# A vision tower with a Mamba block and 16 experts: routing weights by DMA from a small table, multiplied in by GpSimd

## The chip, the cores and the metric

One core of a Trainium2 chip runs the whole program in one launch. The metric is the device time of one execution in microseconds (us). TensorE, VectorE (DVE), ScalarE (ACT), GpSimd (POOL) and SyncE (SP, which here only issues DMAs) each run their own queue in order and meet at semaphores.

## What is computed

The input is 32 images, 36 patches each, so 1152 tokens of 192 features after the patch embedding. A layer norm feeds a Mamba block (input projection with a gate, a selective scan over the 36 tokens of an image with 16 states for each of 384 channels, output projection, then a gated FFN of 512). A second layer norm feeds a mixture of experts:

```python
g = t @ gate_w.T + gate_b
vals, idx = jax.lax.top_k(g, K)            # K = 4 of E = 16
w = jax.nn.softmax(vals, axis=-1) / K
full_w = zeros((T, E)).at[arange(T)[:, None], idx].set(w)
h = einsum('th,ehf->tef', t, w1) + b1
h = _swiglu(h)        # min(glu, 7) * sigmoid(1.702 glu) * (clip(lin) + 1)
y = einsum('tei,eih->teh', h, w2) + b2
out = einsum('teh,te->th', y, full_w) * K
```

All 16 experts are computed for every token; the routing weight is zero for twelve of them. Everything is float32.

## The kernel before, in words

Features lie on the partitions, tokens on the free axis. The tokens are cut into four chunks of 8 images, T = 288 tokens. `schedule()` (L76) writes one order of steps by hand: A is the Mamba part of a chunk, B the experts of the chunk before it, and pieces of B are set ahead of named steps of A (`PIECES_BEFORE`, `DOWNS_BEFORE`). `run` (L360) goes through that order three times over: once with A alone for the first chunk, three times in a hardware loop with A of chunk c and B of chunk c-1, once with B alone for the last chunk. Each engine picks its own steps out of the same order, so an engine's queue is in this order whatever else is ready.

A has a scan of 24 steps of two halves each. A half is: TensorE spreads a row of B over the partitions (`spread`, L576), VectorE multiplies (L974) and scans (L983); GpSimd multiplies both halves of a step by C (`read`, L1212) into one of three buffers, and TensorE sums them (`collect`). A state buffer is used again three steps later.

B works on units. Two experts' 192 channels make three tiles of 128, so there are 24 units; the third of each pair has 64 channels of either expert. A unit has these steps:

- gate and linear: five matmuls each on w1 split in a high and a low part (`experts_up`, L692), the bias and minimum on VectorE (L1104), the bias on ACT, the clip on VectorE (L1112: SBUF to SBUF, in two buffers);
- mix: tanh on ACT, (tanh + 1) * gate on VectorE (L1120: two SBUF inputs, one buffer), the product `glu` with the clipped linear part on GpSimd (L1224: one buffer, so it waits for the unit before to be scaled);
- scale: TensorE copies the routing weights of the unit's expert to all 128 partitions in PSUM by a matmul with a selection matrix (`experts_scale`, L717: `pick_unit` times `mix_parts`), and VectorE multiplies `glu` by it into one of 12 `hid` tiles (L1129).

```python
pieces.append([("gate", u)] + ([("scale", u - 1)] if u else []))
pieces.append([("linear", u), ("mix", u)])
```

Each two units have three `down` steps of fp32 matmuls from `hid` by w2 into sums in PSUM, and `experts_finish` adds them to the residual. The order sets units 0 to 7 before the scan, 8 to 15 in it (the scales in it are of units 7 to 14) and 16 to 23 after it.

Before the units come topk (router logits and the four largest), weights (three transposes, ACT copies to `mix_w`, rounds to the upper rows of `mix_parts`, VectorE puts the rest into its lower rows, L1097) and start. The steps topk, weights, start, unit 0 and gate 1 with scale 0 stand ahead of A's `variance`, in which GpSimd takes the power -1/2 for the norms (`take_roots`, L1165 to L1167), after which VectorE makes `diag` (L915), TensorE spreads it and VectorE scales the features (L924, L927).

SP loads the patches of the next chunk in `center` (L445: 864 KB, into `x_patch`), and w1 of pair e+2 once the last linear of pair e is done (L453: 1152 KB, two buffers); it waits in its queue in the same order. In the first chunk ACT rounds `pick_unit` from a 576 KB load that lies in `hid` until then (L828, L479), and VectorE zeroes the other rows (L1149, L1150).

## Time and profile before

| | us |
|---|---|
| median of 3 runs | 804.27 (803.79 to 808.25) |
| the profiled execution | 805.15 |
| its span in the trace | 803.4 |
| TensorE busy | 634.8 (79%) |
| VectorE busy | 523.8 (65%) |
| ScalarE busy | 275.0 (34%) |
| GpSimd busy | 273.9 (34%) |
| DMA | 65.97 MB, mean 82 GB/s |
| mean granted TensorE clock | 0.881 of 2.4 GHz |

The trace lists every instruction with start and duration, what it waited for, and the clock that TensorE was granted (1.0 or 0.5, that is 2.4 or 1.2 GHz). Matmuls are pipelined, so their durations overlap and their sum is more than they cost; start to start is the measure. All matmuls come from the helper on L488 and all ACT instructions from L751, so they are told apart by the tiles that they write and read. Tiles are named by their first word: `scratch` holds l_raw, g_tanh, g_act, glu, g_min and l_clip. A name such as `pb` is a PSUM tensor.

### The profile page before, as it was taken

To read this page: it belongs to the slowest core of one execution; us is meant where nothing else is said; L and a number is where in the kernel's file an instruction comes from. 1 tells how busy PE (TensorE), PEld (TensorE's weight loads), DVE (VectorE), ACT (ScalarE), POOL (GpSimd) and SP (SyncE) were. 2 spreads that over 40 slices of the span, in tenths; PEclk is the share of its full clock that TensorE was granted. 3 is DMA by queue.
4 is the path that set the end of the run, shared out by engine and by line. 5 is a ranking of instruction groups with operands and counts; after the bars stand their busy time and mean duration, and the time that the engine had idled before them with its cause. 6 is when DMAs were issued, how large, how long until landed. Compare 5 with 4: busy or idle time off the path is not lost.

```text
span 803.4 us, 10289 instructions
## 1 busy us (share of the span) xinstructions
PE 634.8 (79%) x2853; PEld 465.5 (58%) x2853; DVE 523.8 (65%) x1104; ACT 275.0 (34%) x623; POOL 273.9 (34%) x266
## 2 busy tenths in 40 slices
PE   5766566698676889978768788988778788976996
PEld 4443344577554657757545556757655456755774
DVE  4268892246699785545689895555579896555664
ACT  1285451023734322213734231203644341212331
POOL 2437793012244541212145452122135453112322
PEclk8768897889689899979779999979869899987999
DMA  6934351413011011122111011122110110221430
GB/s 202 295 138 140 122 192 59 176 45 110 17 53 60 1 60 60 63 82 89 59 59 59 0 59 59 59 71 103 60 59 1 59 59 18 100 71 59 155 141 11
DMA packets 15153, 65.97 MB, mean 82 GB/s; under 512 B 2464, under 2 KB 7888, under 8 KB 9808
## 3 DMA queue, kind: packets, MB, share of 16 engines
q1 hardware_dynamic: 15104, 65.47, 23.8%
q14 instruction: 38, 0.31, 0.1%
q8 instruction: 11, 0.18, 0.1%
HBM read 55.12 MB, written 10.32 MB: 81 GB/s over the span
## 4 chain that ended last, share of the span: by engine, by line
PE 47%; DVE 27%; issue 11%; ACT 9%; POOL 4%; DVEq 1%; DMA 0%; ACTq 0%; POOLq 0%; SPq 0%
PE pa L488 27%; PE pb L488 20%; DVE state L983 9%; DVE pa L974 4%; DVE dt L959 4%; ACT scratch L751 3%; ACT a_bar L751 3%; POOL scratch L1224 2%; DVE hid L1129 2%; POOL root L1167 2%; ACT ffn L751 1%; DVE scratch L1120 1%; DVE scratch L1112 1%; DVE scratch L1104 1%; ACT c_all L751 1%
## 5 line engine op out<-in xcount | busy, mean ns | idle before, releaser
L488 PE MATMUL pa<-bc_parts,pick_state 128*128 128x288 f32 x256 | 109.4, 469 | 93.8 <-DVE state L983 78.7
L1212 POOL TENSOR_TENSOR read<-state,c_all 128x576 f32<-128x576 f32 x92 | 130.0, 1415 | 155.9 <-DVE state L983 149.9
L1224 POOL TENSOR_TENSOR scratch<-scratch 128x288 f32<-128x288 f32 x96 | 77.1, 803 | 266.0 <-DVE scratch L1120 266.0
L488 PE MATMUL pb<-t_high,w 128*128 128x288 f32 x576 | 156.0, 336 | 4.0 <-DVE scratch L1104 3.9
L983 DVE TENSOR_TENSOR_SCAN state<-a_bar,pa 128x288 f32<-128x288 f32 x192 | 144.3, 751 | 16.0 <-ACT a_bar L751 0.5
L488 PEld LDWEIGHTS pa<-bc_parts,pick_state 128*128 128x128 f32 x256 | 57.1, 226 | 143.4 <-DVE state L983 118.2
L751 ACT ACTIVATE a_bar<-dt,decay 128x280 f32<-128x280 f32 x192 | 97.6, 524 | 111.7 <-DVE state L983 111.7
L488 PE MATMUL pa<-read,ident 128*128 128x288 f32 x384 | 123.1, 449 | 6.0 <-DVE read L991 5.8
L751 ACT ACTIVATE scratch<-pb,vec 128x288 f32<-128x288 f32 x96 | 47.9, 499 | 204.2 <-PE pb L488 204.2
L488 PEld LDWEIGHTS pb<-t_high,w 128*128 128x128 f32 x576 | 106.4, 199 | 19.0 <-DVE scratch L1104 6.1
L488 PE MATMUL pb<-hid,w 128*64 128x288 f32 (+1 forms) x384 | 103.8, 462 | 11.5 <-DVE hid L1129 11.4
L488 PE MATMUL pb<-t_low,w 128*128 128x288 f32 x384 | 112.1, 306 | 0.0
L974 DVE TENSOR_TENSOR pa<-u,pa 128x288 f32<-128x288 f32 x192 | 84.9, 442 | 28.2 <-PE pa L488 28.2
L488 PEld LDWEIGHTS pa<-read,ident 128*128 128x128 f32 x384 | 76.7, 210 | 37.2 <-issue 9.1
L488 PEld LDWEIGHTS pb<-t_low,w 128*128 128x128 f32 x384 | 76.2, 199 | 0.0
L1112 DVE TENSOR_SCALAR scratch<-scratch 128x288 f32<-128x288 f32 x96 | 41.9, 437 | 34.4 <-ACT scratch L751 33.5
L488 PEld LDWEIGHTS pb<-hid,w 128*64 128x64 f32 (+1 forms) x384 | 45.8, 177 | 29.5 <-DVE hid L1129 15.3
L1104 DVE TENSOR_SCALAR scratch<-pb,vec 128x288 f32<-128x288 f32 x96 | 49.2, 512 | 17.6 <-PE pb L488 17.0
L1129 DVE TENSOR_TENSOR hid<-scratch,pb 128x288 f32<-128x288 f32 x96 | 43.0, 448 | 18.4 <-POOL scratch L1224 18.4
L1120 DVE SCALAR_TENSOR_TENSOR scratch<-scratch 128x288 f32<-128x288 f32 x96 | 43.5, 454 | 0.9
L751 ACT ACTIVATE scratch<-scratch 128x288 f32<-128x288 f32 x96 | 41.7, 434 | 6.9 <-DVE scratch L1104 6.9
L751 ACT ACTIVATE gate_tanh<-pa 128x288 f32<-128x288 f32 x28 | 11.5, 410 | 72.0 <-PE pa L488 72.0
(132 smaller groups left out, 741.7 us busy)
## 6 DMA issues: line engine op xcount, KB each, us to landing
w<-w_store SPq DMA_DIRECT2D x32, 1152.0 KB, 5.1
w_store<-w SPq DMA_DIRECT2D x8, 1152.0 KB, 5.0
scratch<-expert_w SPq DMA_DIRECT2D x16, 384.0 KB, 5.6
x_patch<-patches SPq DMA_DIRECT2D x4, 864.0 KB, 4.6
w<-expert_w SPq DMA_DIRECT2D x1, 2304.0 KB, 9.9
x_patch<-patches SPq DMA_DIRECT2D x3, 288.0 KB, 4.1
w_embed<-embed_w SPq DMA_DIRECT2D x3, 256.0 KB, 3.8
hid<-unit_pick SPq DMA_DIRECT2D x1, 576.0 KB, 14.8
```

The costliest lines, as they stand in the source:

```text
L488: return nc.tensor.matmul(out, lhsT, rhs, start=start, stop=stop)
L751: return nc.scalar.activation(out, in_, func, **kw)
L959: dve.scalar_tensor_tensor(dt[:, j, :], factors[:, k, :], rest, product, ALU.add, ALU.mult).then_inc(poly.sem, 1)
L974: dve.tensor_tensor(b_x, u[:, j, :], b_x, ALU.mult).then_inc(bx_ready.sem, 1)
L983: dve.tensor_tensor_scan(state_half(g), a, b_x, 0.0, ALU.mult, ALU.add).then_inc(scanned.sem, 1)
L1104: dve.tensor_scalar(g_min[un % 2], pb[:, GATE, 0:T], col("b1_gate", un), LIMIT, ALU.add, ALU.min)\
L1112: dve.tensor_scalar(l_clip[un % 2], l_raw[un % 2], 1.0 + LIMIT, 1.0 - LIMIT, ALU.min, ALU.max)\
L1120: dve.scalar_tensor_tensor(g_act, g_tanh, 1.0, g_min[un % 2], ALU.add, ALU.mult)\
L1129: dve.tensor_tensor(hid[:, un % HID_TILES, :], glu, pb[:, WEIGHT, 0:T], ALU.mult)\
L1167: pool.tensor_tensor(root[:, 1, :], root[:, 0, :], minus_half[:, :], ALU.pow)\
L1212: pool.tensor_tensor(read[:, i % READ_SLOTS, :], state[:, i % STATE_SLOTS, :], c_pair(i), ALU.mult)\
L1224: pool.tensor_tensor(glu, g_act, l_clip[un % 2], ALU.mult).then_inc(glu_ready.sem, 1)
```

## The change

- SP writes the routing weights, halved by ACT (16 rows of 288), to a small HBM table `mix_rows`, and for each unit reads them back twice with a step of 0: 64 partitions with the row of one expert, 64 with that of the other or the same. Four slots `route_rows`; the load for unit u+4 is issued once unit u is scaled.
- GpSimd, not VectorE, multiplies `glu` by the slot (`experts_scale`), in the same place of the order.
- TensorE's selection matmuls, `pick_unit`, `mix_parts`, their load, rounding and memsets, and one bank of PSUM go.
- TensorE's `start` waits for `mix_w` alone.

The diff without the declarations of tiles and semaphores and the empty entries:

```diff
-                      (w2[:, :, :], expert_w2), (b2[0:EXPERTS, 0:HIDDEN], expert_b2),
-                      (raw_unit, unit_pick))
+                      (w2[:, :, :], expert_w2), (b2[0:EXPERTS, 0:HIDDEN], expert_b2))
...
+            def load_route(un):
+
+                pair, k = divmod(un, 3)
+                slot = un % ROUTE_SLOTS
+                for half in range(2):
+                    e = 2 * pair + (k if k < 2 else half)
+                    sp.dma_start(route_rows[half * REST:(half + 1) * REST, slot, :],
+                                 mix_rows[e:e + 1, :].to_broadcast([REST, T])).then_inc(route_in[slot].sem, 16)
+
+            def experts_start(c, _):
+                sp.wait_ge(mix_halved.sem, mix_halved.at(c, 1))
+                sp.dma_start(mix_rows, mix_half[:, :]).then_inc(mix_kept.sem, 16)
+                sp.wait_ge(mix_kept.sem, mix_kept.at(c, 1))
+                for un in range(ROUTE_SLOTS):
+                    load_route(un)
+
+            def experts_scale(c, un):
+
+                if un + ROUTE_SLOTS < UNITS:
+                    sp.wait_ge(hid_ready.sem, hid_ready.at(c, un + 1))
+                    load_route(un + ROUTE_SLOTS)
...
-                pe.wait_ge(mix_high.sem, mix_high.at(c, 1))
-                pe.wait_ge(mix_low.sem, mix_low.at(c, 1))
...
-            def experts_scale(c, un):
-
-                if un:
-                    pe.wait_ge(hid_ready.sem, hid_ready.at(c, un))
-                mm(pb[:, WEIGHT, 0:T], pick_unit[:, un, :], mix_parts[:, :], True, True).then_inc(pe_weight.sem, 1)
-
...
-            def outproj(c, _):
-                if not after_first(c):
-                    act.wait_ge(load_late.sem, 16 * len(LATE_LOADS))
-                    act.wait_ge(rows_zeroed.sem, 1)
-                    activate(pick_unit[0:MIX_ROWS, :, :], raw_unit, ACT.Copy).then_inc(picks_rounded.sem, 1)
-
...
+                if after_first(c):
+                    for k in range(ROUTE_SLOTS):
+                        act.wait_ge(route_in[k].sem, route_in[k].at(c, 0))
                 act.wait_ge(mix_copied.sem, mix_copied.at(c, 1))
-                activate(mix_parts[0:EXPERTS, :], mix_w[0:EXPERTS, :], ACT.Copy).then_inc(mix_high.sem, 1)
+                activate(mix_half[:, :], mix_w[0:EXPERTS, :], ACT.Copy, scale=0.5).then_inc(mix_halved.sem, 1)
...
-            def experts_weights(c, _):
-
-                dve.wait_ge(mix_high.sem, mix_high.at(c, 1))
-                dve.tensor_tensor(mix_parts[32:32 + EXPERTS, :], mix_w[0:EXPERTS, :], mix_parts[0:EXPERTS, :].bitcast(F32),
-                                  ALU.subtract).then_inc(mix_low.sem, 1)
-
...
-            def experts_scale(c, un):
-
-                dve.wait_ge(glu_ready.sem, glu_ready.at(c, un + 1))
-                dve.wait_ge(pe_weight.sem, pe_weight.at(c, un + 1))
-                if un >= HID_TILES:
-                    dve.wait_ge(pe_hid.sem, pe_hid.at(c, (un - HID_TILES) // 2 + 1))
-                dve.tensor_tensor(hid[:, un % HID_TILES, :], glu, pb[:, WEIGHT, 0:T], ALU.mult)\
-                    .then_inc(hid_ready.sem, 1)
...
-            dve.memset(pick_unit[32:64, :, :].bitcast(F32), 0.0)
-            dve.memset(pick_unit[64:P, :, :].bitcast(F32), 0.0).then_inc(rows_zeroed.sem, 1)
...
+            def experts_scale(c, un):
+
+                pool.wait_ge(glu_ready.sem, glu_ready.at(c, un + 1))
+                slot = un % ROUTE_SLOTS
+                pool.wait_ge(route_in[slot].sem, route_in[slot].at(c, un // ROUTE_SLOTS + 1))
+                if un >= HID_TILES:
+                    pool.wait_ge(pe_hid.sem, pe_hid.at(c, (un - HID_TILES) // 2 + 1))
+                pool.tensor_tensor(hid[:, un % HID_TILES, :], glu, route_rows[:, slot, :], ALU.mult)\
+                    .then_inc(hid_ready.sem, 1)
...
-            pool.memset(mix_parts[:, :].bitcast(F32), 0.0)
```

## Rows read from the trace of the kernel before

**Rows 1.** Windows by stage: length, busy PE, PEld, DVE, ACT, POOL, clock, DMA.
```profile
212.00:300.00 88.00, 68.58 (x287) 48.45 (x288) 76.50 (x141) 33.44 (x73) 40.37 (x33) 0.88 0.12 41
300.00:351.00 51.00, 45.88 (x234) 35.11 (x233) 25.55 (x60) 10.22 (x23) 9.00 (x10) 0.90 0.21 75
...
752.00:776.00 24.00, 24.00 (x145) 18.36 (x144) 13.17 (x31) 6.65 (x16) 6.27 (x8) 1.00 0.40 145
```

**Rows 2.** Groups by line: busy us, mean ns, idle before, its releaser.
```profile
L1224 POOL TENSOR_TENSOR scratch<-scratch 128x288 f32<-128x288 f32 x96 | 77.1, 803 | 266.0 <-DVE scratch L1120 266.0
...
L1129 DVE TENSOR_TENSOR hid<-scratch,pb 128x288 f32<-128x288 f32 x96 | 43.0, 448 | 18.4 <-POOL scratch L1224 18.4
...
L488 PE MATMUL pb<-mix_parts,pick_unit 128*128 128x288 f32 x96 | 30.3, 316 | 0.1
```

**Rows 3.** Timeline in the second pass's scan: start, duration, engine.
```profile
235.76 1.43 POOL L1212 TENSOR_TENSOR read<-state,c_all 128x576 f32<-128x576 f32 x1 [1.17 <-DVE state L983]
...
237.50 0.45 DVE L1129 TENSOR_TENSOR hid<-scratch,pb 128x288 f32<-128x288 f32 x1
237.86 0.75 DVE L983 TENSOR_TENSOR_SCAN state<-a_bar,pa 128x288 f32<-128x288 f32 x1
...
238.77 1.40 POOL L1212 TENSOR_TENSOR read<-state,c_all 128x576 f32<-128x576 f32 x1 [0.83 <-DVE state L983]
```

**Rows 4.** Timeline of the same scan, a little earlier, at L1112.
```profile
231.78 1.41 POOL L1212 TENSOR_TENSOR read<-state,c_all 128x576 f32<-128x576 f32 x1 [4.39 <-DVE state L983]
...
232.10 1.26 DVE L1112 TENSOR_SCALAR scratch<-scratch 128x288 f32<-128x288 f32 x1
```

**Rows 5.** Timeline ahead of the first pass's scan, to GpSimd's power.
```profile
172.64 0.36 SPq L445 DMA_DIRECT2D x_patch<-patches  x1
...
173.31 0.44 ACT L751 ACTIVATE mix_parts<-mix_w 16x288 fp32r<-16x288 f32 x1
...
178.41 0.80 POOL L1224 TENSOR_TENSOR scratch<-scratch 128x288 f32<-128x288 f32 x1 [13.32 <-DVE scratch L1120]
...
179.91 1.33 POOL L1167 TENSOR_TENSOR root<-root,minus_half 96x6 f32<-96x6 f32 x1 [0.70 <-DVE root L911]
```

**Rows 6.** DMA issues: count, KB each, median us from issue to landing.
```profile
w<-w_store SPq DMA_DIRECT2D x32, 1152.0 KB, 5.1
...
x_patch<-patches SPq DMA_DIRECT2D x4, 864.0 KB, 4.6
...
out_main<-result SPq DMA_DIRECT2D x4, 144.0 KB, 1.8
...
b<-expert_b SPq DMA_DIRECT2D x1, 12.0 KB, 12.5
```

**Rows 7.** Timeline behind the power: the spread roots and L924.
```profile
182.09 1.24 PE L488 MATMUL pa<-diag,ones 96*128 96x288 f32 x4 [1.59 <-DVE diag L915]
...
183.90 0.75 DVE L924 TENSOR_TENSOR y<-centered,pa 128x576 f32<-128x576 f32 x1
```

**Rows 8.** Timeline with B alone, light units: products, and matmuls of a run.
```profile
740.14 0.80 POOL L1224 TENSOR_TENSOR scratch<-scratch 128x288 f32<-128x288 f32 x1 [1.16 <-DVE scratch L1120]
...
742.10 0.80 POOL L1224 TENSOR_TENSOR scratch<-scratch 128x288 f32<-128x288 f32 x1 [1.16 <-DVE scratch L1120]
742.12 0.30 PE L488 MATMUL pb<-t_high,w 128*128 128x288 f32 x1
...
742.25 0.29 PE L488 MATMUL pb<-t_low,w 128*128 128x288 f32 x1
```

**Rows 9.** Timeline at the start of B alone.
```profile
729.00 0.44 ACT L751 ACTIVATE mix_parts<-mix_w 16x288 fp32r<-16x288 f32 x1
...
730.28 2.26 PE L488 MATMUL pb<-mix_w,b 128*128 128x288 f32 x4 [1.75 <-DVE mix_parts L1097]
```

**Rows 10.** Timeline at the last unit of a chunk.
```profile
344.00 3.44 PE L488 MATMUL pb<-hid,w 128*128 128x288 f32 x8 [2.72 <-DVE hid L1129]
```

**Rows 11.** Waits: us in total, times, longest.
```profile
DVE pa L974 <- PE pa L488: 28.2, 10, 6.0
```

More of the change, by code:

```diff
@@ L46 @@
 HID_TILES = 12
+ROUTE_SLOTS = 4
 PAD_LOGIT = -3.0e38
@@ L186, in vit_tower @@
         decay_rows = sb("decay_rows", [NJ * GROUPS_PER_BLOCK, P])
-        pick_unit = sb("pick_unit", [P, UNITS, P], F32R)
         pick_state = sb("pick_state", [P, 2, P], F32R)
@@ L244, in vit_tower @@
         mix_w = sb("mix_w", [P, T])
-        mix_parts = sb("mix_parts", [P, T], F32R)
+        mix_half = sb("mix_half", [EXPERTS, T])
+        route_rows = sb("route_rows", [P, ROUTE_SLOTS, T])
         HALF = PAIR_COLS // 2
@@ L262, in vit_tower @@
         pa = ctx.enter_context(nc.psum_tensor("pa", [P, 3, 512], F32))
-        pb = ctx.enter_context(nc.psum_tensor("pb", [P, 5, 512], F32))
-        GATE, LINEAR, WEIGHT, SUM, SUM_REST = range(5)
+        pb = ctx.enter_context(nc.psum_tensor("pb", [P, 4, 512], F32))
+        GATE, LINEAR, SUM, SUM_REST = range(4)
+        mix_rows = nc.dram_tensor("mix_rows", [EXPERTS, T], F32).ap()
         w1_store = nc.dram_tensor("w1_store", [PAIRS, P, 3, PAIR_COLS], F32).ap()
@@ L339, in vit_tower @@
         mix_copied = signal("mix_copied", 1)
-        mix_high = signal("mix_high", 1)
-        mix_low = signal("mix_low", 1)
+        mix_halved = signal("mix_halved", 1)
+        mix_kept = signal("mix_kept", 1, 16)
+        route_in = [signal(f"route_in{k}", UNITS // ROUTE_SLOTS, 32) for k in range(ROUTE_SLOTS)]
         w1_in = [signal(f"w1_in{k}", PAIRS // 2, 16) for k in range(2)]
@@ L345, in vit_tower @@
         pe_linear = signal("pe_linear", UNITS)
-        pe_weight = signal("pe_weight", UNITS)
         linear_copied = signal("linear_copied", UNITS)
@@ L378, in vit_tower @@
         raw_state = result[0:64, 0, 0:2 * P].rearrange("p (k n) -> p k n", k=2)
-        raw_unit = hid[0:MIX_ROWS, :, :].rearrange("p a t -> p (a t)")[:, 0:UNITS * P]\
-            .rearrange("p (n m) -> p n m", n=UNITS)
         def scan_half(g):
@@ L480, in _ @@
             run(sp, {"split_w1": split_w1, "center": center,
+                     "experts_start": experts_start, "experts_scale": experts_scale,
                      "experts_linear": experts_linear, "experts_finish": experts_finish})
@@ L659, in scale3 @@
                 if not after_first(c):
-                    pe.wait_ge(picks_rounded.sem, 2)
                     pe.wait_ge(bias_raised.sem, 1)
@@ L744, in _ @@
                 "experts_start": experts_start, "experts_gate": experts_gate,
-                "experts_linear": experts_linear, "experts_scale": experts_scale,
-                "experts_down": experts_down})
+                "experts_linear": experts_linear, "experts_down": experts_down})
         @block.scalar
@@ L889, in _ @@
                 "broadcast": broadcast, "square": square, "log1p": log1p,
-                "split_w1": split_w1, "decay": decay_step, "outproj": outproj,
+                "split_w1": split_w1, "decay": decay_step,
                 "variance2": variance2, "ffn": ffn_gate_tanh, "center3": center3, "scale3": scale3,
@@ L1147, in _ @@
             dve.memset(w_ffn_rest[REST:P, :, :], 0.0)
-            dve.memset(w_router_rest[REST:P, :], 0.0)
-            dve.memset(pick_unit[32:64, :, :].bitcast(F32), 0.0)
-            dve.memset(pick_unit[64:P, :, :].bitcast(F32), 0.0).then_inc(rows_zeroed.sem, 1)
+            dve.memset(w_router_rest[REST:P, :], 0.0).then_inc(rows_zeroed.sem, 1)
             dve.wait_ge(load_embed.sem, 16 * len(EMBED_LOADS))
@@ L1158, in _ @@
                 "variance3": variance3, "scale3": scale3, "experts_topk": experts_topk,
-                "experts_weights": experts_weights, "experts_gate": experts_gate,
-                "experts_linear": experts_linear, "experts_mix": experts_mix,
-                "experts_scale": experts_scale, "experts_finish": experts_finish})
+                "experts_gate": experts_gate,
+                "experts_linear": experts_linear, "experts_mix": experts_mix, "experts_finish": experts_finish})
         @block.gpsimd
@@ L1244, in _ @@
                 "variance2": lambda c, _: take_roots(c, 2), "variance3": lambda c, _: take_roots(c, 3),
-                "split_w1": split_w1, "drive_u": drive_u, "read": read_states, "outproj": outproj, "scale3": scale3, "experts_mix": experts_mix})
+                "split_w1": split_w1, "drive_u": drive_u, "read": read_states, "outproj": outproj, "scale3": scale3, "experts_mix": experts_mix,
+                "experts_scale": experts_scale})
 def _twice(w):
```

## The prediction

> **What bounds the kernel now.** I read the windows by stage first [rows 1]. From the second pass of the order on, one chunk's Mamba part (A) runs beside the experts (B) of the chunk before it; a pass of the loop is a pre-scan stretch (47 us), the scan (88 us) and a post-scan stretch (50 us), and after three passes B runs alone (about 80 us). The busiest engine differs. In the scan VectorE is busy 76.5 of 88.0 us and TensorE 68.6; in the post-scan stretch TensorE is busy 45.9 of 51 and VectorE half; with B alone TensorE fills the middle (24.0 of 24.0 us) and shares the first 16 us with a ring of waits. So the two removed instructions pay in different places: VectorE's multiply in the scans, TensorE's matmul elsewhere. GpSimd is busy 40.4 of 88 us in the scan, 9 of 51 after it.
>
> The groups by line [rows 2] give sizes: VectorE's multiply L1129 448 ns (96 times, 43.0 us), GpSimd's product of the same shape L1224 803 ns, the selection matmul 316 ns (30.3 us). None of these totals is a gain. Two matmuls of one run start 0.13 us apart [rows 8], so at the upper clock one matmul in a stream costs 0.13 us, not 0.316.
>
> **The scan, VectorE's multiply (the largest term).** In the timeline [rows 3] L1104 starts at 237.08, L1129 at 237.50, the scan step L983 at 237.86: L1129 adds 0.36 us to a queue that hardly pauses. A scan holds 8 scales (units 7 to 14) in each of three passes: 24 x 0.36 = **-8.6 us**. The new cover is GpSimd's. Its `read` lasts 1.4 us; the scale comes behind a `read` and ahead of the next, and reads are 3.0 us apart there [rows 3], 2.65 once VectorE loses 0.36: 1.41 + 0.80 + 0.08 = 2.3 fits. If it didn't, the next read would come late, and VectorE only needs it three steps later. Where `drive_u` also stands there (twice a pass) the read is half a microsecond late, which I cost at nothing for the same reason. Ends: 0 (another engine ends each cycle) and -0.45 each (its whole duration), -10.8.
>
> **The port between VectorE and GpSimd.** The trace shows a cost that no busy total does. L1112 reads and writes SBUF and takes 0.30 us, but 1.26 us where a `read` had begun 0.32 us before it: it ends 0.17 us after GpSimd does [rows 4]. L1129, with one operand in PSUM, is 441 to 456 ns in all its 96 executions [rows 4]. The Trainium skill, GPSIMD Engine Reference, "Key points", says that GpSimd shares its SBUF interfaces with VectorE and contends with instructions in a 2-port mode or with two SBUF inputs; by that rule doubling GpSimd's work speaks against this change, and it is the slow rival below. The trace agrees with it at L1112.
>
> Where does a scale meet L1112 or L1120? In the scan the read ahead of L1112 is already there and the scale lies three halves away: nothing. With B alone it is unavoidable. Now the ring is L1120, product, L1129, L1112, L1120, 1.96 us a unit (740.14 to 742.10 [rows 8]). After the change GpSimd does 0.80 + 0.80 with about 0.08 between its instructions, and VectorE's L1112 and L1120 must fit between: 1.76 us with no exclusion, 0.80 + 0.80 + 0.30 + 0.45 = 2.35 if all four are serial. About 2.1 is likely, since starts overlap. The load of the next w1 pair, 5.1 us from issue to landing [rows 6], now stands on SP behind a wait for the scale and two small loads, and hid under three units (5.9 us) with 0.8 us to spare; that adds a little. Nine light units at +0.19: **+1.7 us**, ends -1.8 and +3.5.
>
> **TensorE's matmul.** The post-scan stretch is TensorE-bound from the out-projection to the FFN's down-projection; about 7 selections lie in it: 3 x 7 x 0.13 = -2.7. Before the scan one lies on the path in each pass: -0.4. B alone has 7 in the full middle and 8 at its end: -2.0. Together **-5.1 us**; at 1.2 GHz each would be 0.24, and if every one is hidden 0. The wait of a selection for the multiply before it goes too; it is inside the ring above.
>
> **The start of B.** `mix_parts` is gone, and with B alone its chain shows: ACT starts it at 729.00 when mix_w is ready, VectorE follows, TensorE starts at 730.28 [rows 9]. Without both, TensorE starts 0.36 us behind mix_w: **-0.95 us**, once. In the loop TensorE is busy there: 0.
>
> **L1129 ahead of A's work.** At 183.53 it stands in front of L924, which starts at 183.90, though TensorE had its operand at 183.33 [rows 7]. Three passes at 0.5: **-1.5 us**. Elsewhere before the scan A waits for ScalarE, and nothing is won.
>
> **The table's way out and back.** GpSimd's queue is now product 0, scale 0, power (L1167), and the power is on A's path. The product ends at 179.2, the power starts at 179.91 [rows 5]; scale 0 alone takes the time to 180.1. But scale 0 needs the table: ready on ACT at 173.75, written to HBM behind the patches, whose load (864 KB) is issued at 172.64 [rows 5] and takes 4.6 us [rows 6]. A small transfer behind a large one waits: 12 KB took 12.5 us behind 2304 KB, where 144 KB alone took 1.8 [rows 6]. So written about 177.5, eight reads issued, the first rows about 179.7, scale 0 to 180.6: the power is 0.8 us late in each pass. SP, which stands at that write, has nothing else due. **+2.4 us**, ends +0.6 (rows in time) and +7.5 (2.5 us late each). With B alone there are 7 us for two transfers of about 2: hidden. Later rows are asked for three units ahead, over 5 us: hidden, unless directly behind a w1 load.
>
> **The last unit.** Where TensorE waits for the last hidden tile (344.00, for L1129 [rows 10]) the product-to-tile time goes from 0.03 + 0.45 to 0.08 + 0.80: +0.4 us, four chunks, **+1.6 us**, plus two such waits inside the end of B alone, +0.6.
>
> **First chunk.** It loses a 576 KB load, an ACT copy, two VectorE and one GpSimd memset. They run beside TensorE's embedding and the scan; at worst they are a small gain. 0.
>
> **Sum**: -8.6 - 5.1 - 0.95 - 1.5 + 1.7 + 2.4 + 1.6 + 0.6 = -9.85 us. The profiled execution took 805.15 us (span 803.4); that gives 795.3. The median of the runs is 0.9 below the profiled one, so I forecast **794.5 us**. The new traffic, 192 loads of 72 KB (13.8 MB beside 66), is costed only in the w1 term.
>
> **Rivals.**
> - *TensorE or the waits take over in the scan.* VectorE's 0.36 is swallowed because TensorE ends the cycle (68.6 of 88 us busy, and part of each scan is at the lower clock). The -8.6 shrinks to about -2: 801. Against it: before the scan's multiply L974 VectorE idles for TensorE ten times in all, 28.2 us, up to 6.0 us each, so at the starts of the scans and almost never within them [rows 11]. With late tables on top, 803 to 806. Chance 0.17.
> - *More is freed.* VectorE idles 18.4 us for products that it then multiplies [rows 2]; if two fifths of it come back as A's progress, another -7: 787. For it: in-order VectorE couples A to B at every L1129. Against: most of that idle is in B's own ring. Chance 0.18.
> - *The port decides (slower).* If each scale in the scans drifts to stand ahead of L1112, as the reads do, VectorE pays up to 0.80 - 0.36 = +0.44 on 24 units instead of -0.36: +19.2 on the forecast, 813 to 814. It decides from the point where GpSimd's queue is more than about 1 us behind at `linear`. The reads' slack of a third of a microsecond speaks against it; the 0.3 to 1.26 us spread of L1112 shows how much a small shift does. By the page's rule alone, with no look at positions, it would be the likeliest. Chance 0.08.
> - *The change doesn't reach the path*: the rows come in time but the clock or the order gives it all back, within 0.5%. Counted in the first rival.
>
> Forecast itself: 0.57, between 789 and 799.5. The range reaches into the second rival and most of the first: 785.5 to 803. By cases: faster by over 0.5% (4.0 us, about what a measurement of this kernel can tell from no change) 0.57 + 0.18 and 0.04 of the first rival, 0.79; within 0.13; slower 0.08.
>
> **What would show it.** Scan stretches shorter by about 3 us each, L983 starting 0.36 sooner after L1104, L1112 no longer than now in them; L1167 about 0.8 us later against the embedding, released by the scale and that by a DMA; with B alone a ring of 2.0 to 2.2 us with L1112 or L1120 stretched; first-unit products 1 us earlier there. Wrong: scans as long as now (first rival), L1120 at 1 us or more in them (third), or table rows that GpSimd waits for in mid-chunk.

## The result: 0.5% slower, and the profile after

The changed kernel takes **810.34 us** (median of 11 runs, 809.37 to 812.47), the kernel before 806.65 us beside it (803.79 to 808.41). The ratio is **1.0051, 95% interval 1.0035 to 1.0067**. The forecast of 794.5 us, faster, is wrong in sign and outside its range.

The two traced executions differ by more than the medians do, 7.3 us against 3.7: the one of the kernel before (805.15 us) is quicker than its median, and the one of the changed kernel (812.47 us) is the slowest of its eleven. So about half of the differences below belongs to these two executions, and a single stretch is to be trusted only where its cause is seen.

The page of the changed kernel, its first part, then busy by engine, DMA, and the two DMA issues that matter (count, KB each, median us to landing):

```profile
span 810.7 us, 10333 instructions
...
PE 633.1 (78%) x2757; PEld 463.0 (57%) x2757; DVE 493.2 (61%) x1002; ACT 272.9 (34%) x622; POOL 351.1 (43%) x361
...
DMA packets 30577, 79.62 MB, mean 98 GB/s; under 512 B 5584, under 2 KB 23360, under 8 KB 25280
...
w<-w_store SPq DMA_DIRECT2D x32, 1152.0 KB, 5.2
route_rows<-mix_rows SPq DMA_DIRECT2D x192, 72.0 KB, 2.7
```

The groups by line (busy us, mean ns, idle before, releaser):

```profile
L1223 POOL TENSOR_TENSOR hid<-scratch,route_rows 128x288 f32<-128x288 f32 x96 | 77.7, 809 | 13.5 <-DMA route_rows<-mix_rows 6.1 <-POOL scratch L1214 2.9
...
L1114 DVE TENSOR_SCALAR scratch<-scratch 128x288 f32<-128x288 f32 x96 | 46.9, 489 | 44.2 <-ACT scratch L762 42.8
...
L1122 DVE SCALAR_TENSOR_TENSOR scratch<-scratch 128x288 f32<-128x288 f32 x96 | 48.5, 505 | 2.7 <-ACT scratch L762 1.8
```

The work moved as intended. The scale is L1223 on GpSimd, 96 x 809 ns, where it was L1129 on VectorE, 448 ns [rows 2]. L1114 and L1122 are the old L1112 and L1120; they grew from 437 and 454 ns to 489 and 505. GpSimd waits for table rows only 6.1 us in the whole run.

Windows, the same columns as [rows 1]: the second pass's scan and post-scan stretch, then B alone:

```profile
212.00:300.00 88.00, 69.71 (x283) 47.83 (x282) 75.01 (x133) 35.91 (x80) 46.73 (x41) 0.88 0.17 55
300.00:351.00 51.00, 44.35 (x225) 33.53 (x226) 22.61 (x53) 10.24 (x23) 15.82 (x19) 0.91 0.26 89
...
736.00:752.00 16.00, 10.43 (x59) 9.31 (x59) 10.50 (x18) 5.17 (x12) 9.60 (x12) 0.82 0.58 168
752.00:776.00 24.00, 23.38 (x133) 18.62 (x133) 11.56 (x25) 6.82 (x17) 12.82 (x16) 0.94 0.55 190
```

With B alone TensorE is busy 10.43 of the 16 us from 736 to 752; in the kernel before it was 15.48. (B alone starts 3.2 us later in the changed kernel; moved by that, from 739.2 to 755.2, it is 10.43 too.) That is one place of the loss. To find all of them I cut both timelines at the same events. `power` is GpSimd's L1157 (L1167 before); it runs three times a chunk, and the first stands ahead of the scan. Sums over the three passes of the loop, in us:

| | start of embedding to power 1 | power 1 to scan | scan | scan end to power 2 | power 2 to 3 | power 3 to next embedding | B alone |
|---|---|---|---|---|---|---|---|
| before | 45.4 | 100.6 | 253.7 | 29.1 | 94.7 | 40.2 | 74.8 |
| after | 50.9 | 103.3 | 248.3 | 28.7 | 91.7 | 43.8 | 78.9 |
| difference | +5.5 | +2.7 | -5.4 | -0.4 | -2.9 | +3.6 | +4.1 |

They add up to +7.2; the other 0.1 us of 810.7 - 803.4 lies ahead of the first pass. The gains expected in the scan and behind it are there, 8.3 us. Four stretches lose 16. A second trace of the changed kernel (8 below) gives +7.3, +3.2, -5.9, -0.4, -1.9, +3.6 and +3.8 against the same trace of before: the signs and the order of size hold.

**Before power 1.** The first pass, on GpSimd, SP and the engines behind them (start, duration, idle before in brackets):

```profile
173.49 0.44 ACT L762 ACTIVATE mix_half<-mix_w 16x288 f32<-16x288 f32 x1
173.95 0.32 SPq L465 DMA_DIRECT2D mix_rows<-mix_half  x1
...
177.62 6.23 SPq L460 DMA_DIRECT2D route_rows<-mix_rows  x10
178.12 0.81 POOL L1214 TENSOR_TENSOR scratch<-scratch 128x288 f32<-128x288 f32 x1 [12.33 <-DVE scratch L1122]
178.61 0.15 DVE L919 TENSOR_SCALAR root<-pa 96x3 f32<-96x3 f32 x1
...
181.29 0.79 POOL L1223 TENSOR_TENSOR hid<-scratch,route_rows 128x288 f32<-128x288 f32 x1 [2.36 <-DMA route_rows<-mix_rows]
182.04 1.33 POOL L1157 TENSOR_TENSOR root<-root,minus_half 96x6 f32<-96x6 f32 x1
183.40 0.76 DVE L923 TENSOR_TENSOR diag<-ident,root 96x576 f32<-96x576 f32 x1 [4.65 <-POOL root L1157]
184.21 2.29 PE L509 MATMUL pa<-diag,ones 96*128 96x288 f32 x4 [4.28 <-DVE diag L923]
```

VectorE's roots are ready by 178.9, GpSimd stands 2.36 us at the rows of the table, and the power starts at 182.04. TensorE then waits 4.28 us for `diag`; before it waited 1.59 [rows 7]. The same four matmuls take 2.29 us instead of 1.24. The windows say why (columns as above):

```profile
182.00:188.00 6.00, 3.79 (x12) 3.22 (x13) 3.23 (x7) 0.26 (x1) 2.95 (x4) 0.50 0.27 71
188.00:200.00 12.00, 11.98 (x61) 9.94 (x61) 5.56 (x14) 4.35 (x12) 4.71 (x6) 0.98 0.39 136
```

The granted clock is 0.50 from 182 to 188, 1.2 GHz: it falls at about 181.7, within TensorE's longer wait, and is back at 1.00 about 6.8 us later. In the kernel before it is 1.00 throughout from 168 to 205. This happens in each of the three passes.

### The profile page after: what moved, and what is told of

It reads as the page before. It is cut to its first block, busy times and chain, and to the rows that moved or that the text cites. A ratio compares the mean times of both kernels' runs of the same rounds, so it can differ in the third digit from the quotient of the medians.

```text
span 810.7 us, 10333 instructions
## 1 busy us (share of the span) xinstructions
PE 633.1 (78%) x2757; PEld 463.0 (57%) x2757; DVE 493.2 (61%) x1002; ACT 272.9 (34%) x622; POOL 351.1 (43%) x361
## 2 busy tenths in 40 slices
DMA packets 30577, 79.62 MB, mean 98 GB/s; under 512 B 5584, under 2 KB 23360, under 8 KB 25280
## 4 chain that ended last, share of the span: by engine, by line
PE 50%; DVE 25%; issue 9%; ACT 8%; POOL 4%; DMA 1%; DVEq 1%; POOLq 0%; ACTq 0%; SPq 0%
PE pa L509 30%; PE pb L509 20%; DVE state L991 9%; DVE dt L967 4%; DVE pa L982 4%; ACT scratch L762 3%; ACT a_bar L762 2%; POOL root L1157 2%; POOL scratch L1214 2%; DVE scratch L1122 1%; POOL hid L1223 1%; ACT ffn L762 1%; DMA w<-w_store 1%; ACT c_all L762 1%; DVE scratch L1114 1%
## 5 line engine op out<-in xcount | busy, mean ns | idle before, releaser
L509 PE MATMUL pb<-t_high,w 128*128 128x288 f32 x576 | 159.3, 343 | 8.8 <-DVE scratch L1106 4.9
L991 DVE TENSOR_TENSOR_SCAN state<-a_bar,pa 128x288 f32<-128x288 f32 x192 | 144.2, 751 | 15.9 <-ACT a_bar L762 0.5
L509 PE MATMUL pa<-read,ident 128*128 128x288 f32 x384 | 125.9, 457 | 6.0 <-DVE read L999 5.8
L509 PEld LDWEIGHTS pb<-t_high,w 128*128 128x128 f32 x576 | 109.6, 205 | 24.2 <-issue 5.8
L509 PE MATMUL pb<-t_low,w 128*128 128x288 f32 x384 | 114.4, 311 | 0.0
L1223 POOL TENSOR_TENSOR hid<-scratch,route_rows 128x288 f32<-128x288 f32 x96 | 77.7, 809 | 13.5 <-DMA route_rows<-mix_rows 6.1
L509 PEld LDWEIGHTS pb<-t_low,w 128*128 128x128 f32 x384 | 78.2, 204 | 0.0
L1114 DVE TENSOR_SCALAR scratch<-scratch 128x288 f32<-128x288 f32 x96 | 46.9, 489 | 44.2 <-ACT scratch L762 42.8
L1106 DVE TENSOR_SCALAR scratch<-pb,vec 128x288 f32<-128x288 f32 x96 | 49.1, 512 | 19.5 <-PE pb L509 18.7
L1122 DVE SCALAR_TENSOR_TENSOR scratch<-scratch 128x288 f32<-128x288 f32 x96 | 48.5, 505 | 2.7 <-ACT scratch L762 1.8
L509 PE MATMUL pa<-diag,ones 96*128 96x288 f32 x40 | 22.7, 710 | 20.7 <-DVE diag L923 20.7
```

The source lines that it names most:

```text
L509: return nc.tensor.matmul(out, lhsT, rhs, start=start, stop=stop)
L991: dve.tensor_tensor_scan(state_half(g), a, b_x, 0.0, ALU.mult, ALU.add).then_inc(scanned.sem, 1)
L1106: dve.tensor_scalar(g_min[un % 2], pb[:, GATE, 0:T], col("b1_gate", un), LIMIT, ALU.add, ALU.min)\
L1114: dve.tensor_scalar(l_clip[un % 2], l_raw[un % 2], 1.0 + LIMIT, 1.0 - LIMIT, ALU.min, ALU.max)\
L1122: dve.scalar_tensor_tensor(g_act, g_tanh, 1.0, g_min[un % 2], ALU.add, ALU.mult)\
L1223: pool.tensor_tensor(hid[:, un % HID_TILES, :], glu, route_rows[:, slot, :], ALU.mult)\
```

## Experiments

Eleven kernels besides one repeat of the changed one. Each ratio is against the kernel before on the same chip. Experiments 1 to 4 ran on one chip, 5 and 7 to 11 on a second, 6 and 12 on a third, so between these groups the ratios compare better than the medians. Diffs are cut to the edit.

**1. GpSimd's power ahead of the scale.** In the loop the scale of unit 0 is issued behind the power, so that no power waits for the table.

```diff
-                "scale": scale, "variance": lambda c, _: take_roots(c, 1),
+                "scale": scale, "variance": variance,
...
+            def variance(c, _):
+                take_roots(c, 1)
+                if after_first(c):
+                    experts_scale(c - 1, 0, held=True)
...
+                if un == 0 and after_first(c) and not held:
+                    return
```

> One move in GpSimd's queue: inside the loop the power for the norms comes before scale 0, not behind it. Theory T (the table comes late and the power waits behind scale 0, which then also lets TensorE's clock fall): the power is back at 14.4 to 15.0 us after the pass's embedding begins (now 17.0), each of the three passes is 2.5 to 3 us shorter, and the kernel takes 802 to 803.5, at or under the kernel before; the stretch with B alone stays at 79 us. Rival P (the port and GpSimd's longer instruction in mid-chunk cost it): the power moves but the passes get at most 1 us shorter each, 808 to 810.

Measured: 793.39 us, **ratio 0.9826 [0.9792, 0.9860]**. One edit of order turns 0.5% slower into 1.7% faster. The direction was expected; the gain is twice the 7 to 8 us that I had given it. Its timeline:

```profile
179.00 0.80 POOL L1219 TENSOR_TENSOR scratch<-scratch 128x288 f32<-128x288 f32 x1 [14.26 <-DVE scratch L1122]
179.75 1.33 POOL L1157 TENSOR_TENSOR root<-root,minus_half 96x6 f32<-96x6 f32 x1
181.12 0.75 DVE L923 TENSOR_TENSOR diag<-ident,root 96x576 f32<-96x576 f32 x1 [1.48 <-POOL root L1157]
181.92 1.24 PE L509 MATMUL pa<-diag,ones 96*128 96x288 f32 x4 [1.13 <-DVE diag L923]
182.17 0.94 POOL L1230 TENSOR_TENSOR hid<-scratch,route_rows 128x288 f32<-128x288 f32 x1 [1.08 <-DMA route_rows<-mix_rows]
```

The scale still waits 1.08 us for the table, but nobody waits for it. TensorE waits 1.13 us instead of 4.28, and the matmuls take 1.24 us again. Against the changed kernel, over the three passes, embedding to power gives back 7.4 us, power to scan 5.0, power 3 to the next embedding 1.5, the rest 1.2: 15.1. B alone is unchanged (78.7).

**2. VectorE multiplies, from the DMA rows.** L1223 moves back to VectorE; the table and its loads stay.

```diff
+                dve.tensor_tensor(hid[:, un % HID_TILES, :], glu, route_rows[:, slot, :], ALU.mult)\
+                    .then_inc(hid_ready.sem, 1)
```

> Only the engine is undone: VectorE multiplies again, from the rows that the DMA brought (two SBUF inputs); tables and loads stay. Theory T: the rows are as late, VectorE waits for them ahead of the variance's steps, so the power is late as now (16.5 to 17.5 us behind the embedding), the scans lose their gain (84 to 85.5 us) and the last units gain 0.4 us: 812 to 816. Rival P: with GpSimd back at half its work the kernel comes to 804 to 807.

Measured: 813.38 us, 1.0067 [1.0040, 1.0094]. The scans are back at 254.2 us in all (253.7 before), and VectorE now is the engine at which the table arrives late. From its groups by line:

```profile
L1134 DVE TENSOR_TENSOR hid<-scratch,route_rows 128x288 f32<-128x288 f32 x96 | 44.3, 461 | 25.3 <-POOL scratch L1227 16.6 <-DMA route_rows<-mix_rows 8.7
```

The scan's gain belongs to the move to GpSimd, and the loss ahead of the scan to the table: embedding to power is 50.9 us here too.

**3. No trip through HBM.** The write of the table and the wait for it go; the rows are read from an input that is always there. This kernel leaves out the routing weights: the hidden tiles are multiplied by other numbers.

```diff
-                sp.dma_start(mix_rows, mix_half[:, :]).then_inc(mix_kept.sem, 16)
-                sp.wait_ge(mix_kept.sem, mix_kept.at(c, 1))
...
-                                 mix_rows[e:e + 1, :].to_broadcast([REST, T])).then_inc(route_in[slot].sem, 16)
+                                 patches[0][e:e + 1, 0, :].to_broadcast([REST, T])).then_inc(route_in[slot].sem, 16)
```

> Leaves out the write of the table to HBM and the wait for it; the rows are read from an input instead (values of the patches stand in for the routing weights). Loads, their number and everything behind stay. Theory T: rows come 3.5 us earlier, the power is at 15.0 to 15.4 us behind the embedding, no drop of the clock there, each pass 2 us shorter, 803 to 805; B alone still loses time at w1 if SP's issues are what delays it (77 to 79 us). Rival P: 808 or more.

Measured: 801.68 us, 0.9924 [0.9897, 0.9951]. Embedding to power falls to 45.2 us, as in the kernel before. So the wait for the table is the whole +5.5. The clock did fall, though, which the expectation had ruled out: TensorE still waits 2.1 us for `diag`, and the clock behind it is 0.50 for 6.8 us in the first pass and 3.4 in the others. The stretch behind the power stays at 102.5, and the kernel is 8 us slower than experiment 1, where the scale itself is out of the way too.

**4. Selection matmul kept, GpSimd multiplies.** From the kernel before: ScalarE copies the selection's result to SBUF (two buffers) and GpSimd multiplies from it. No DMA.

```diff
+                activate(route_rows[:, un % 2, :], pb[:, WEIGHT, 0:T], ACT.Copy).then_inc(weight_copied.sem, 1)
...
+                pool.tensor_tensor(hid[:, un % HID_TILES, :], glu, route_rows[:, un % 2, :], ALU.mult)\
+                    .then_inc(hid_ready.sem, 1)
```

> The other half alone: the selection matmul stays as before, ACT copies its result to SBUF (0.4 us a unit more on ACT, two buffers), GpSimd multiplies. No table, no row loads. Theory T: scans 2 us shorter than before, the power 0.3 us late, B alone without the stall for w1 (75 to 77 us): 799 to 803, faster than before by 0.5%. Rival P: the cost is GpSimd's, so it is as slow as the changed kernel, 809 to 812.

Measured: 809.05 us, 1.0020 [1.0004, 1.0035]. Missed: I had expected a gain. The new copy is a wait of its own:

```profile
L1231 POOL TENSOR_TENSOR hid<-scratch,route_rows 128x288 f32<-128x288 f32 x96 | 76.6, 798 | 90.1 <-ACT route_rows L753 52.4 <-issue 31.5 <-POOL scratch L1223 3.2
```

The scans are 251.1 us, 2.6 below before, and power 2 to power 3, where TensorE and ScalarE feed the FFN, grows from 94.7 to 98.3. So moving the multiply to GpSimd doesn't pay here once ScalarE has to bring the weights to SBUF. It is not a clean test of the move alone.

**5. A late power in the kernel before.** GpSimd does five 128x160 products on spare tiles ahead of the power.

```diff
+                if n == 1 and after_first(c):
+                    for k in range(5):
+                        pool.tensor_tensor(spare[:, k, :], spare_in[:, :], spare_in[:, :], ALU.mult)
```

> The kernel before, with only GpSimd's power made late: in each pass of the loop five small products on spare tiles (about 2.6 us, no other use) stand between the product of unit 0 and the power. No table, no moved multiply. Theory T (a late power is the whole loss of the passes, its own delay and a fall of TensorE's clock that it brings): the power is at 16.5 to 17 us behind the embedding instead of 15, the clock falls for some 7 us right behind it, and the stretch from the power to the scan becomes about 1 us longer; 3 x 2.5 to 3: 815 (812 to 818), slower by 0.9 to 1.3%. Rival D (what costs is the table's loads and SP, the delay of the power is absorbed): at most 810.

Measured: 808.10 us, 1.0019 [0.9994, 1.0044]. Missed, though the delay was smaller than meant: the five products take 2.10 us, part of it beside a wait, and the stretch to the power grows by 1.3 us a pass (45.4 to 49.3). The clock behaves as theory T had it, 0.50 behind the power for 3.4 us in the first pass and 6.8 in the others, and power to scan grows by 4.1 us in all. The time hardly moves even so.

**6. A longer one.** Two powers on a spare tile, 2.62 us.

```diff
+                if n == 1 and after_first(c):
+                    for k in range(2):
+                        pool.tensor_tensor(spare[:, k, :], spare_in[:, :], minus_half[:, :], ALU.pow)
```

> The delay of e_late_power again, now of the changed kernel's own size: in the kernel before, two powers on a spare tile (2.66 us) stand ahead of the power in each pass, which puts it about 1.85 us later. e_late_power held it back by 1.28 us, lengthened the two stretches around the power by 1.3 and 0.7 to 1.7 us and gave back most of that in the scan and behind it. If a late power is most of the changed kernel's loss: those two stretches 1.8 and 0.6 to 1.8 us longer in each pass, a fall of the clock right behind the power in all three, 810 to 813 (0.4 to 0.8% slower than before). If the loss needs the table's traffic too: 1.002 again, 808 to 809.

```profile
178.60 2.62 POOL L1170 TENSOR_TENSOR spare<-spare_in,minus_half 96x6 f32<-96x6 f32 x2
...
181.20 1.32 POOL L1172 TENSOR_TENSOR root<-root,minus_half 96x6 f32<-96x6 f32 x1
```

Measured: 807.01 us, 1.0001 [0.9982, 1.0019]. Missed again. The two stretches come out as in the changed kernel, 50.9 and 103.3 us, +8.1 together. Yet the time is unchanged: power 2 to 3 gives back 1.9, power 3 to embedding 1.4, the scans 0.8, B alone 2.0. So the price of a late power is paid in this kernel too and comes back elsewhere, and the next run asks what it does in the changed one.

**7. The same delay in the kernel of experiment 1**, where the table is out of the power's way: the lines of 6 and those of 1.

```diff
+                        pool.tensor_tensor(spare[:, k, :], spare_in[:, :], minus_half[:, :], ALU.pow)
...
+                take_roots(c, 1)
+                if after_first(c):
+                    experts_scale(c - 1, 0, held=True)
```

> e_power_first with the delay put back by other means: two powers on a spare tile (2.66 us) ahead of the power in each pass, which put it at 16.5 to 17 us behind the embedding as in the changed kernel, with scale 0 still behind it. If the changed kernel loses its 15 us against e_power_first by the late power alone, this kernel is back at 807 to 811, with the stretch from the power to the scan at 34 to 34.6 us again. If the kernel can absorb it, as the kernel before did with e_later_power, and the loss needs scale 0 and its table ahead of the power: 796 to 801.

```profile
177.12 2.62 POOL L1160 TENSOR_TENSOR spare<-spare_in,minus_half 96x6 f32<-96x6 f32 x2
...
179.71 1.32 POOL L1162 TENSOR_TENSOR root<-root,minus_half 96x6 f32<-96x6 f32 x1
181.00 0.79 POOL L1235 TENSOR_TENSOR hid<-scratch,route_rows 128x288 f32<-128x288 f32 x1
```

Measured: **811.66 us**, 1.0066 [1.0040, 1.0093]; the changed kernel itself, run beside it (**8**), 811.08 us, 1.0057 [1.0029, 1.0085]. The delay owes nothing to the table, since the power here stands ahead of everything that waits for rows. It takes back all that the order had won: 2.4% by the ratios, 18 us by the medians. The expectation for the repeat:

> The changed kernel unaltered, on the same chip as the other, so that the two can be compared: 1.003 to 1.007 of the kernel before, about 810.

The clock behind the power, in the windows of experiment 1 and then of this kernel:

```profile
180.00:186.00 6.00, 4.50 (x26) 3.61 (x25) 4.49 (x10) 1.67 (x4) 4.05 (x5) 1.00 0.50 109
```

```profile
180.00:186.00 6.00, 3.54 (x11) 2.97 (x12) 3.57 (x7) 0.02 (x1) 3.37 (x4) 0.50 0.33 71
```

**9. One DMA for a unit of one expert** (16 of 24 units; the others need two).

```diff
+                if k < 2:
+                    e = 2 * pair + k
+                    sp.dma_start(route_rows[:, slot, :], mix_rows[e:e + 1, :].to_broadcast([P, T]))\
+                        .then_inc(route_in[slot].sem, 16)
+                    return
```

> The changed kernel, but one DMA instead of two for the 16 of 24 units with one expert: SP issues 32 loads a chunk, not 48. Theory S (SP's 0.64 us for each issue delays both the first rows and, with B alone, the load of w1): the power 0 to 0.6 us earlier in each pass, the wait for w1 with B alone 1 to 2.5 us instead of 3.9: 805 to 808. Rival B (the transfers themselves, not their issue, are late): within 1 us of the changed kernel, 809 to 811.

Measured: 807.93 us, 1.0023 [0.9999, 1.0047]. B alone shrinks from 78.9 to 76.6 us; the passes hardly move. The wait of TensorE for w1 falls from 3.88 to 2.49 us. The numbers are those of theory S, the reason isn't: the w1 load is issued 11.75 us after B alone begins, in the changed kernel 11.74. It lands sooner, 5.75 us after its issue instead of 7.15, which is nearer to rival B's reason.

**10. Experiments 1 and 9 together**, by both of their diffs.

> The two edits together: power ahead of scale 0 in the loop, one load for a unit with one expert. Theory S: what the first edit gave plus 1.5 to 3 us with B alone: 790 to 792. Rival B: 793 to 794.

Measured: 792.14 us, **0.9830 [0.9785, 0.9876]**. The profiled span is 789.0 us against 794.9 for experiment 1, 3.9 of it in B alone. But the medians differ by 1.3 only, and the ratios (0.9830, 0.9826) not at all: no gain over experiment 1 is shown.

**11. As 10, and VectorE multiplies the last unit of a chunk**, from the same rows.

```diff
-                if un == 0 and after_first(c) and not held:
+                if un == 0 and after_first(c) and not held or un == UNITS - 1:
                     return
```

> The same, and VectorE multiplies in the last unit of each chunk, where TensorE waits for it. If GpSimd's longer instruction costs there what the timeline shows (0.4 us a chunk), four chunks give 1.5 us more: 788.5 to 790.5. If VectorE's two SBUF inputs or the clock take that back, no difference.

Measured: 791.65 us, 0.9822 [0.9784, 0.9861]. No gain over 10 that can be told: GpSimd's longer product at the chunk's end isn't what costs there.

**12. As 10, but GpSimd multiplies only units 7 to 14**, those in the scan, and VectorE the rest, unit 0 behind its roots.

```diff
-                if un == 0 and after_first(c) and not held:
+                if not 7 <= un <= 14:
                     return
```

> From f_power_one_load: GpSimd multiplies only in units 7 to 14, those of the scan; VectorE multiplies the others from the same rows, in unit 0 of a pass after the roots. If GpSimd's multiply is worth its place only where VectorE's queue is full: B alone 1 to 2 us shorter (ring 1.96 again) and the rest even, 789 to 791. If VectorE's multiply ahead of A's steps is what the changed kernel was right to remove everywhere: passes 0.5 to 1 us longer each, 793 to 795.

Measured: 793.83 us, 0.9850 [0.9815, 0.9884]. B alone is the shortest of the table kernels, 71.7 us, but each pass pays about a microsecond ahead of the scan, where VectorE's multiply is on A's path again (power to scan 101.2 against 98.3).

## Why the prediction was wrong

**The step that failed is "The table's way out and back".** I priced a power 0.8 us late in each pass at +2.4 us, with +7.5 as the upper end. Two things were wrong in it.

*The size of the delay.* I expected the first rows at 179.7. They landed at 180.14 and 181.22, since unit 0 needs two DMAs, the second is issued 0.52 us behind the first (the later ones follow 0.64 apart, the row of the timeline above: 10 in 6.23 us; x_patch took SP 0.36 [rows 5]) and each takes 2.5 to 3.1 us. Embedding to power grew by 5.5 us in three passes, 1.8 a pass. Experiment 3 shows that the trip is all of this.

*What a late power costs.* I counted its own lateness. But TensorE idled 4.28 us for it, the granted clock fell to 0.5 within that wait and stayed there for 6.8 us, and power to scan grew by a further 2.7 us. The clock's share can be read from passes of one kernel: with the delay of experiments 5 and 6 this stretch takes 34.1 to 34.2 us where the clock is low for 3.4 us behind the power and 35.0 to 35.3 where it is low for 6.8, against 33.5 with no fall. Experiment 1 against the changed kernel puts the whole bill at 12.4 us in those two stretches and about 17 us in the medians. Experiment 7 puts the bill back (154.7 us in the two stretches, the changed kernel 154.2, experiment 1 141.8) with work that has nothing to do with the table. So in this kernel a late power is enough for the loss, whoever makes it late. Experiment 6, where it costs nothing in total, says that something else in the changed kernel is needed for it; port, table and traffic are not excluded as that condition. With the power first those two stretches are even 4.2 us shorter than before the change (141.8 against 146.0). The terms of L1129 ahead of A's work (-1.5) and of the selection (-0.4) account for less than half of that; the late power had hidden it all.

How much hangs on this one step: without its +2.4 the forecast would have been 792.1 us, and experiment 1, with the power out of the table's way, takes 793.4. That is partly luck, since there the two stretches around the power gain more than forecast (-4.2 against -1.9) and B alone loses 4 us that I had not counted.

What stays **open** is why the same delay is free in the kernel before. The granted clock goes with it. Trace: time at clock 0.5 in us; runs: median of the mean granted clock of all executions:

| kernel | trace | runs |
|---|---|---|
| before | 194 | 0.873 or 0.874 (17 to 23 beside the experiments) |
| 5, before with a delay | 195 | 0.882 |
| 6, before with a longer one | 186 | 0.887 |
| 1, power first | 204 | 0.872 |
| 10, power first, one load | 187 | 0.879 |
| 7, power first, with the delay | 217 | 0.865 |
| changed, two traces | 232, 238 | 0.859 |

The kernel before alone ranges from 799.41 us at a mean clock of 0.890 to 809.63 us at 0.869 (23 executions beside experiment 7). A line through the 17 beside experiment 6 gives 3.3 us for each 0.01 of clock; by this estimate the 0.013 that experiment 6 has more than they have returns about 4 us of the 8.1 that its two stretches cost. So the delay isn't free there: the clock is higher elsewhere and pays half of it or so. In the table kernels the same delay brings a lower clock instead. In experiment 6 the clock is low behind the power for 3.4, 6.8 and 3.4 us, in 7 and in the changed kernel for 6.8 in every pass; and the end of a chunk is low for 13.7 us in the first two passes of the changed kernel where it was 10.2 before. TensorE has 96 matmuls less to bridge its waits there. Their absence alone doesn't lower the clock (experiment 10). That the two together do fits the table above, but the kernels with the table also have its traffic and, all but one, GpSimd's multiply, and no run separates these; it is argued only.

**The scan** was right in mechanism and too large in sum. Here is the place of [rows 3] one pass later:

```profile
272.67 0.51 DVE L1106 TENSOR_SCALAR scratch<-pb,vec 128x288 f32<-128x288 f32 x1
272.74 0.79 POOL L1223 TENSOR_TENSOR hid<-scratch,route_rows 128x288 f32<-128x288 f32 x1
273.09 0.74 DVE L991 TENSOR_TENSOR_SCAN state<-a_bar,pa 128x288 f32<-128x288 f32 x1
...
274.00 1.41 POOL L1202 TENSOR_TENSOR read<-state,c_all 128x576 f32<-128x576 f32 x1 [0.47 <-DVE state L991]
```

L991 starts 0.42 us after L1106 started, and the distance between scan steps there is 1.44 instead of 1.80: the 0.36 of the sum, at seven of the eight places of a pass (1.57 at the eighth), and the read is in time. But 24 x 0.36 = 8.6 became 5.4. The rest went back at other steps. The largest that comes back in each pass is a scale that meets VectorE's products on `dt`. Changed kernel, then the same place before:

```profile
257.48 3.02 DVE L967 SCALAR_TENSOR_TENSOR dt<-ffn,dt 128x288 f32<-128x288 f32 x3
...
258.69 1.00 POOL L1223 TENSOR_TENSOR hid<-scratch,route_rows 128x288 f32<-128x288 f32 x1
```

```profile
255.24 2.55 DVE L959 SCALAR_TENSOR_TENSOR dt<-ffn,dt 128x288 f32<-128x288 f32 x3
```

The three products took 2.55 us and take 3.02, and the scale beside them takes 1.00 instead of 0.79. I had looked for meetings with L1112 and L1120 only, and those cost too: in the three scans L1114 and L1122 are busy 3.0 us more than L1112 and L1120 were (33.6 against 30.6). With the products on `dt` that is enough for the missing 3.2 us, though not all of it need lie on the path. So that step of the prediction ("nothing") was wrong for both, and the first rival, which had TensorE swallow the gain, isn't what happened either.

**TensorE's matmul**: right. Power 2 to power 3 is 2.9 us shorter where I had -2.7; in passes with the clock at 1.00 throughout it is 29.96 us against 30.94. In B's full middle, products are 3.13 us apart, before 3.26: 0.13 each.

**The start of B**: right. From the start of the copy that ScalarE makes behind `mix_w` (`mix_half`, before `mix_parts`) to GpSimd's first product it is 6.17 us, before 7.24: -1.07, where I had -0.95.

**B alone**: the ring was right, the load of w1 was not. This is the ring, with what stands around the load of w1 on SP:

```profile
741.56 0.81 POOL L1223 TENSOR_TENSOR hid<-scratch,route_rows 128x288 f32<-128x288 f32 x1
...
742.40 1.08 SPq L460 DMA_DIRECT2D route_rows<-mix_rows  x2
...
742.76 0.80 POOL L1214 TENSOR_TENSOR scratch<-scratch 128x288 f32<-128x288 f32 x1 [0.39 <-DVE scratch L1122]
...
743.53 0.58 SPq L451 DMA_DIRECT2D w<-w_store  x1
743.64 0.80 POOL L1223 TENSOR_TENSOR hid<-scratch,route_rows 128x288 f32<-128x288 f32 x1
743.67 1.09 DVE L1122 SCALAR_TENSOR_TENSOR scratch<-scratch 128x288 f32<-128x288 f32 x1
...
744.84 0.80 POOL L1214 TENSOR_TENSOR scratch<-scratch 128x288 f32<-128x288 f32 x1 [0.39 <-DVE scratch L1122]
...
750.72 0.61 PE L509 MATMUL pb<-t_high,w 128*128 128x288 f32 x1 [3.88 <-DMA w<-w_store]
```

A unit takes 2.08 us where I had said 2.0 to 2.2. L1122 is stretched to 1.09 us: it starts 0.03 us behind the scale and ends 0.32 behind it, so the two barely overlap. The Trainium skill, GPSIMD Engine Reference, "Key points", says that GpSimd contends with VectorE's instructions that take two inputs from SBUF. The trace agrees, and adds the size.

The miss is the last row: TensorE stands 3.88 us for w1. The load could go once the last linear matmul of unit 2 is done. In the kernel before it does, at once:

```profile
738.34 0.30 PE L488 MATMUL pb<-t_low,w 128*128 128x288 f32 x1
...
738.67 0.34 SPq L453 DMA_DIRECT2D w<-w_store  x1
```

In the changed kernel that matmul ends at 740.38 and the load is issued at 743.53, 3.15 us later. SP stood at the scale of unit 1, which ends at 742.37, and then issued the two loads behind it (742.40). The eight first rows, 4.9 us of issues, were out by then, and with fewer of them experiment 9 issues the load no sooner. The load also lands 7.15 us after its issue, before 5.03. Counted from the start of B alone (728.57 and 731.79) the issue is 1.6 us later and the landing another 2.1. The forecast had named just this place, "behind a wait for the scale and two small loads", and given it no number of its own ("adds a little"). From the first product to the seventh B now takes 16.5 us, before 11.7: +4.8, where the term for all nine light units was +1.7. The middle gives back 0.8, the start 1.1, the end takes 1.1 more, and the whole of B is +4.1.

**The last unit**: the 0.4 us is there (342.34 to 343.19, 0.85 from the start of the scale to the matmul instead of 0.51), but the stretch grew by 3.6 us in three passes, not 1.2. TensorE idles 3.72 us ahead of it where it was 2.72 [rows 10]; a third of that is the longer scale and a third the selection matmul, which used to end 0.33 us behind the last matmul that is now ahead of the wait. The larger part is the clock. Experiment 1 shows it within one trace, on the same instructions: the stretch takes 13.12 us in the first pass, where the clock is 0.50 for 9.9 us of it, and 11.63 in the second, where it is for 6.8. The changed kernel takes 13.13 in both (9.8 us at 0.50), the kernel before 11.48 and 11.82 (6.8 and 6.7). Why the clock is low longer is not shown. Experiment 11 finds no gain in a shorter scale there.

The slow rival, the port deciding in the scans, gave 813 to 814 us, near the time measured, for a reason that the scans refute: they are shorter. A right number doesn't save the mechanism.

By the sum: scan -8.6 measured -5.4; post-scan -2.7, -2.9; table +2.4, +8.2 in its two stretches (with the -1.9 of L1129 and the selection inside); B alone -0.25 net, +4.1; chunk's end +1.2, +3.6; scan end to power 2, not in the sum, -0.4. That is +7.2, in the traces; the medians have half of it. Two slips in the working change nothing: two waits at 0.4 us are 0.8, not 0.6, and 192 loads of 72 KB are 14.2 MB by the profile's count, not 13.8.

## What to carry to other kernels

When work moves to an in-order queue, ask first what stands behind it there, and put the short instruction that an idle TensorE waits for ahead of anything that waits for a DMA; here that one order is worth 2.2% and decides the sign. Price a delay of the critical engine not by its length but with what its clock does behind it, and when the answer is unknown, give it a wide bound. Treat the DMA queue as an in-order engine too: a large load behind a wait and two small loads was issued 3.2 us after it could have been, and it landed 2.1 us slower among small ones. Halving the small loads of most units gave the changed kernel 2 to 3 us; on top of experiment 1 no gain is shown.

Four versions beat both kernels, experiments 1, 10, 11 and 12, the same within their intervals: 0.983, 0.983, 0.982 and 0.985 of the time before.

## What the runs showed of the hardware that I had not expected

- A load of 72 KB that repeats one row over 64 partitions holds SP's queue for 0.64 us a piece, a plain 1152 KB load 0.58 beside it and 0.32 in the kernel before. The size of a transfer doesn't set its time on the issuing queue.
- With the row loads the packets double (30577 against 15153 before), for 18% of the bytes (14.2 of 79.6 MB). The w1 load issued at 743.53 landed at 750.67, 7.1 us, where the median is 5.2.
- About 2.7 us more idle time of TensorE ahead of `diag` (4.28 against 1.59) went with a granted clock of 0.50 for 6.8 us, from within the wait on, and the four matmuls behind it took nearly twice as long (2.29 against 1.24 us).
- The same 2.62 us of foreign work ahead of the same power cost 0.0% in one kernel and 2.4% in another (ratios 1.0066 and 0.9826) that has the table, GpSimd's multiply and no selection matmuls. A cost measured by adding a delay holds for the kernel in which it was measured.
- The kernel before, unchanged and on one chip, took from 799.41 to 809.63 us in 23 executions, with mean granted clocks from 0.890 down to 0.864. Two single traces can differ by as much as the change does.
